# Table pieces behind the tile's transfers, and the second layer's first operand by halves

## The reference, cut to what matters

```python
# x: (128, 64, 1024) f32
x = x + L0_ffn(einsum('bct,bcd->bdt', x, W0[ids0]))     # 64x64 matrix for each batch entry, then
#   L0_ffn(y) = y @ W_base.T + b_base + 2 * sum_e gate_e * (y @ A_e.T) @ B_e.T   (top 2 of 8 experts, rank 16)
x = x + L1_ffn(x @ W1.T + base_bias + (x @ A[ids1].T) @ B[ids1].T)   # one of 32 adapters a batch entry, rank 16
#   L1_ffn(r) = fp8(r / s_in) @ fp8(Wf / s_w) * (s_in * s_w) + bias2
```

## Time and profile before

| | us |
|---|---|
| median of 3 runs | 2020.85 (2020.4 to 2025.44) |
| the profiled execution | 2019.35 |
| its span, first to last instruction | 2017.5 |
| PE busy | 1983.1 (98%) |
| DVE, POOL, ACT busy | 1490.1, 517.5, 393.9 |

### The profile page before, as it was taken

One profiled execution on the slowest core, in us unless ns is written; L12 is line 12 of the kernel. 1 busy time (PEld: TensorE's weight loads), 2 busy tenths in 40 slices (PEclk: granted clock), 3 DMA queues, 4 the chain that ended last, 5 costly groups with the idle time before them and its releaser, 6 DMA issues.

```text
span 2017.5 us, 38464 instructions
## 1 busy us (share of the span) xinstructions
PE 1983.1 (98%) x13056; PEld 1802.5 (89%) x13056; DVE 1490.1 (74%) x3882; ACT 393.9 (20%) x1084; POOL 517.5 (26%) x469
## 2 busy tenths in 40 slices
PE   6899999999999999999999999999999999999998
PEld 5889999999999999999988888888888888888887
DVE  6887877777766666666657777777777777777777
ACT  3112111111211111111112121212121222122211
POOL 3655411111111111111112222322232223222222
PEclk8999999999999999999999999999999999999999
DMA  7764443343333333333455566566656665665564
GB/s 241 226 192 140 135 122 107 104 126 116 101 111 110 98 97 116 106 96 113 123 162 151 163 166 161 152 168 164 163 148 173 160 161 149 173 159 161 155 171 111
DMA packets 220202, 289.93 MB, mean 144 GB/s; under 512 B 97795, under 2 KB 169477, under 8 KB 220166
## 3 DMA queue, kind: packets, MB, share of 16 engines
q1 hardware_dynamic: 220166, 289.56, 50.7%
HBM read 163.62 MB, written 109.05 MB: 135 GB/s over the span
## 4 chain that ended last, share of the span: by engine, by line
PE 93%; SPq 2%; DMA 2%; POOL 1%; DVE 1%; issue 0%; ACT 0%; DVEq 0%; ACTq 0%
PE bank_g L977 13%; PE bank_g L1032 12%; PE bank_g L979 12%; PE bank_g L978 12%; PE bank_g L1031 12%; PE bank_g L1030 12%; PE bank_f L1040 11%; PE bank_f L957 3%; PE bank_g L1075 1%; PE bank_g L1005 1%; PE bank_g L1006 1%; PE bank_g L1004 1%; DMA raw<-b 1%; DMA raw<-a 1%; POOL w1h L557 1%; POOL w1l L559 1%
## 5 line engine op out<-in xcount | busy, mean ns | idle before, releaser
L977 PE MATMUL bank_g<-w0h,st_h 128*128 128x384 f32 (+1 forms) x1536 | 529.7, 345 | 10.4 <-DMA wpair<-wc 6.5
L978 PE MATMUL bank_g<-w0l,st_h 128*128 128x384 f32 (+1 forms) x1536 | 520.7, 339 | 0.0
L979 PE MATMUL bank_g<-w0h,st_l 128*128 128x384 f32 (+1 forms) x1536 | 520.6, 339 | 0.0
L1030 PE MATMUL bank_g<-w1h,st_h 128*128 128x352 f32 x1536 | 506.1, 329 | 4.0 <-DVE st_l L882 4.0
L1032 PE MATMUL bank_g<-w1h,st_l 128*128 128x352 f32 x1536 | 496.7, 323 | 0.0
L1031 PE MATMUL bank_g<-w1l,st_h 128*128 128x352 f32 x1536 | 495.8, 323 | 0.0
L882 DVE TENSOR_TENSOR st_l<-xbuf,st_h 128x512 fp32r<-128x512 f32 x128 | 212.8, 1703 | 183.9 <-ACT st_h L676 183.9
L977 PEld LDWEIGHTS bank_g<-w0h,st_h 128*128 128x128 f32 x1536 | 289.5, 188 | 41.2 <-issue 26.1
L547 POOL TENSOR_TENSOR xbuf<-xbuf,b_base_sb 128x1024 f32<-128x1024 f32 x64 | 154.4, 2412 | 654.0 <-PE bank_f L957 640.4
L1030 PEld LDWEIGHTS bank_g<-w1h,st_h 128*128 128x128 f32 x1536 | 289.2, 188 | 11.9 <-DVE st_l L882 4.6
L1031 PEld LDWEIGHTS bank_g<-w1l,st_h 128*128 128x128 f32 x1536 | 289.0, 188 | 1.6
(11 more groups left out here) (79 smaller groups left out, 1988.8 us busy)
## 6 DMA issues: line engine op xcount, KB each, us to landing
xbuf<-x SPq DMA_DIRECT2D x64, 512.0 KB, 3.9
x_scratch<-x1buf SPq DMA_DIRECT2D x64, 512.0 KB, 2.9
x1t_scratch<-x_blocks SPq DMA_DIRECT2D x256, 128.0 KB, 2.3
xbuf<-x1t_scratch SPq DMA_DIRECT2D x64, 512.0 KB, 3.6
x1buf<-x_scratch SPq DMA_DIRECT2D x64, 512.0 KB, 5.1
out<-obuf SPq DMA_DIRECT2D x64, 512.0 KB, 2.7
b_stack<-b_split SPq DMA_DIRECT2D x384, 64.0 KB, 3.6
raw<-a_split SPq DMA_DIRECT2D x128, 128.0 KB, 4.2
```

What stands on the lines that cost most here:

```text
L977: pe.matmul(to, st_h[:, rows], w0h[:, k, cols], start=(k == 0), stop=False)
L978: pe.matmul(to, st_h[:, rows], w0l[:, k, cols], start=False, stop=False)
L979: last = pe.matmul(to, st_l[:, rows], w0h[:, k, cols], start=False, stop=(k == KC - 1))
L1030: pe.matmul(to, st_h[:, rows], w1h_k[:, k, cols], start=(k == 0), stop=False)
```

## The change

- `POOL_PIECES_A_TILE` is 2 instead of 3. In SP's loop `tile(t)` comes first and `feed(t)` behind it. The tables now take tiles 0 to 8 and the weight tiles 8 to 20.
- `base_bias` becomes a 17th table piece ("C", 128x8): POOL splits it in stage 1, SP stores it as `bias_split` in DRAM and loads both rows with one DMA to each `b_stack`. `bias_raw`, `bias_h`, `bias_l`, L471, L483 and the operations of ACT (L683) and DVE (L926) go.
- `st_used[h]` is counted in stage 2 too, at the last matmul of each half of k in group 2; ACT waits for it half by half instead of for `main_done`.
- `turned_lo(0, 0, h)` is done inside DVE's last stage 1 tile: half 0 ahead of the additions into `x1buf`, half 1 behind the first of them.
- POOL waits for `bias2` inside its `tile`, behind `fill_slot`.

```diff
-POOL_PIECES_A_TILE = 3
+POOL_PIECES_A_TILE = 2
...
+    bias_dram = nc.dram_tensor("bias_split", (2, D), F32, kind="Internal").ap()
...
+            pool_units += [("C", 0, 0)]
             tables = len(pool_units)
...
+                elif kind == "C":
+                    src = base_bias.rearrange("(p c) -> p c", p=P)
+                    to = [bias_dram[s].rearrange("(p c) -> p c", p=P) for s in range(2)]
...
                 for t in range(PREP_TILES):
+                    tile(t, t % 2, True)
                     feed(t)
-                    tile(t, t % 2, True)
...
-                sp.dma_start(bias_raw[:, :], base_bias.rearrange("(a n) -> a n", a=1)).then_inc(bias_loaded, 16)
+                for b in range(2):
+                    sp.dma_start(b_stack[b][3 * LR:STACK, :].bitcast(F32), bias_dram).then_inc(bias_rows, 16)
...
-                sp.wait_ge(bias_split, 2)
-                for b in range(2):
-                    for s, part in enumerate((bias_h, bias_l)):
-                        sp.dma_start(b_stack[b][3 * LR + s:3 * LR + s + 1, :].bitcast(F32),
-                                     part[:, :].bitcast(F32)).then_inc(bias_rows, 16)
...
-                pool.wait_ge(x1_done[2], TILES)
-                pool.wait_ge(bias2_loaded, 16)
                 def tile(t, b, x1_loads, a_loads, stored):
                     if a_loads is not None:
                         fill_slot(t + 1, 1 - b, a_loads)
+                    if stored is None:
+                        pool.wait_ge(x1_done[2], TILES)
+                        pool.wait_ge(bias2_loaded, 16)
...
-                        act.wait_ge(main_done, t)
                     for h in range(2):
+                        act.wait_ge(st_used[h], TILES + t)
                         act.activation(turned(st_h[:, :], h), in_blocks(xbuf[:, b, :], h), ACT.Copy)\
                            .then_inc(hi_done[h], 1)
...
                     if more:
                         st_lo(n, 0)
+                    else:
+                        turned_lo(0, 0, 0)
...
                         if g == 0 and more:
                             st_lo(n, 1)
+                        elif g == 0:
+                            turned_lo(0, 0, 1)
...
+                        if g == 2 and k % (KC // 2) == KC // 2 - 1:
+                            last.then_inc(st_used[k // (KC // 2)], 1)
...
-                        pe.wait_ge(bias_rows, 64)
+                        pe.wait_ge(bias_rows, 32)
```

More of the change, by code:

```diff
@@ L236, in pool_places @@
                     to = [b1_dram[u * P:(u + 1) * P, s, v * HALF:(v + 1) * HALF] for s in range(2)]
+                elif kind == "C":
+                    src = base_bias.rearrange("(p c) -> p c", p=P)
+                    to = [bias_dram[s].rearrange("(p c) -> p c", p=P) for s in range(2)]
+                    cols = slice(n * HALF, n * HALF + D // P)
+                    return src, D // P, w1h[:, cols], w1l[:, cols], to
                 else:
@@ L265, in build @@
             bias2_sb = sb("bias2_sb", [P, D], F32, p2)
-            bias_raw = sb("bias_raw", [1, D], F32, p2)
-            bias_h = sb("bias_h", [1, D], F32R, p2)
-            bias_l = sb("bias_l", [1, D], F32R, p2)
             x1_loaded = [sem(f"x1_loaded{b}") for b in range(2)]
@@ L274, in build @@
             bias2_loaded = sem("bias2_loaded")
-            bias_loaded = sem("bias_loaded")
-            bias_split = sem("bias_split")
             bias_rows = sem("bias_rows")
@@ L279, in build @@
             turned_loaded = [sem(f"turned_loaded{b}") for b in range(2)]
-            main_done = sem("main_done")
             masked_done = sem("masked_done")
@@ L668, in turned_hi @@
                     act.wait_ge(turned_loaded[b], 16 * loads)
-                    if isinstance(t, int) and t == 0:
-                        act.wait_ge(st_used[1], TILES)
-                    else:
-                        act.wait_ge(main_done, t)
                     for h in range(2):
+                        act.wait_ge(st_used[h], TILES + t)
                         act.activation(turned(st_h[:, :], h), in_blocks(xbuf[:, b, :], h), ACT.Copy)\
@@ L679, in _ @@
                 turned_hi(0, 0, 1)
-                act.wait_ge(x1_done[2], TILES)
-                act.wait_ge(bias_loaded, 16)
-                act.activation(bias_h[:, :], bias_raw[:, :], ACT.Copy).then_inc(bias_split, 1)
                 def tile(t, b, lag, loads):
@@ L753, in _, with turned_lo @@
                 dve.wait_ge(s_scale, 3)
+                def turned_lo(t, b, h):
+                    dve.wait_ge(hi_done[h], TILES + t + 1)
+                    dve.tensor_tensor(turned(st_l[:, :], h), in_blocks(xbuf[:, b, :], h),
+                                      turned(st_h[:, :], h), ALU.subtract).then_inc(lo_done[h], 1)
                 def quantize_weight(u):
@@ L877, in quantize @@
                        .then_inc(rq_done, 1)
[L879 to L884, removed]
                 def finish(t, b, bank=bank_f):
@@ L917, in tile @@
                     if more:
-                        turned_lo(t + 1, 1 - b)
-                turned_lo(0, 0)
+                        for h in range(2):
+                            turned_lo(t + 1, 1 - b, h)
                 dve.wait_ge(ones_set, 1)
                 dve.tensor_copy(ht[3 * LR:STACK, :], ones[3 * LR:STACK, :].to_broadcast([2, P])).then_inc(ht_ones, 1)
-                dve.wait_ge(bias_split, 1)
-                dve.tensor_tensor(bias_l[:, :], bias_raw[:, :], bias_h[:, :], ALU.subtract).then_inc(bias_split, 1)
                 tile(0, 0, 0, True)
@@ L1063, in main @@
                         last.then_inc(h1_ps, 1)
-                    if g == 2:
-                        last.then_inc(main_done, 1)
                 def stacks_in(t, b, loads):
```

## The result

The changed kernel takes 2014.34 us (median of 6 runs, 2011.4 to 2015.59) beside 2021.38 for the one before (6 runs, 2020.4 to 2025.44): a ratio of 0.996, with a 95% interval of 0.9947 to 0.9972. That is 7.0 us won where 13.7 were forecast, outside the range on record. The two profiled executions differ by less still: 2015.41 with a span of 2013.2 against 2019.35 and 2017.5, 4.3 us of span.

What follows compares the result with a forecast made beforehand. PE bounds the kernel, busy 1983.1 of 2017.5 us, so only its idle time and slow stretches can be won. The terms 8.99 - 0.3 + 5.0 = 13.7 us gave 2007.2 us, with a range of 2004 to 2013.

Steps and rivals of the forecast that it cites:

- Stage 1, what is removed: Stage 1, tiles 2 to 5: PE's waits for `wpair` and the slow restarts go, 8.99 us gained.
- Rival A: Stage 1: matrices late from table traffic, not order; 1 us a tile lost over 8 tiles, 2015; chance 0.12.
- Rival B: Stage 1: each of 9 tiles with table traffic costs 2.25 us, so the kernel is slower, 2027; chance 0.04.
- Stage 1, what is added: Stage 1, tiles 8 to 9: POOL waits for the last table piece's store; 0.3 us lost once (0 to 1.0).
- rival D: Stage 1: no effect worth measuring, waits go elsewhere, such as to `xb_done`; 2018 to 2021; chance 0.06.
- (1) to (3): Between the stages: PE gains 2.5 us at its start, 3.3 by L1075, 4.5 by tile 1, 6.1 with the clock.
- (4): Start of `ffn(0)`: a new wait of about 0.9 us for `rqt`; of 6.1 us gained 5.0 are kept.
- (3): Stage 2, tile 1: starts at 1026.8 instead of 1031.33, gain 4.5 us; 6.1 with the clock staying up.
- rival C: Between the stages: adapter B or transpose late, or clock falls; only 1 to 2.5 of 5.0 us stay, 2010.5; chance 0.14.

Runs made afterwards that it cites:

- the hold in all tiles: Changed kernel with POOL's pieces and next bias addition held in each tile until DVE has made `hwt`; 2007.15 us, ratio 0.9929 to the kernel before.
- after_again: The changed kernel run once more, unaltered; 2014.76 us, ratio 0.9971 to the kernel before.
- rest_alone: Changed kernel with three pieces a tile and `feed(t)` first, as before the change; 2019.16 us, ratio 0.9986 to the kernel before.

## Why the prediction was half right

**Stage 1, what is removed: right.** T(5) - T(1) is 61.82, forecast 61.3; 8.47 of 8.99. SP's queue in tile 1 of the changed kernel, T(1) being 58.29:

```profile
60.66 0.35 SPq L411 DMA_DIRECT2D x_scratch<-x1buf  x1
61.06 0.43 SPq L414 DMA_DIRECT2D xbuf<-x  x1
62.87 1.75 SPq L351 DMA_DIRECT2D wpair<-wc  x2
64.67 2.04 SPq L421 DMA_DIRECT2D x1t_scratch<-x_blocks  x4
66.75 0.46 SPq L398 DMA_DIRECT2D a_split<-w1h  x1
```

The store is at T + 2.4 as in the earlier trace rows, the second matrix load is out by T + 6.3, the table's stores stand behind L421. Rival A is out: the landing of `wpair` in this stretch is 2.3 (it was 2.8 in the earlier trace rows), so most of its slowness went with the order, and there is no matrix wait left to give back. The estimate by the Trainium skill (DMA: Bandwidth & Descriptors, on latency), from HBM's access time at high load, was a landing of 3.9; the 2.3 does not bear it out. Rival B needed 1.6 us of lateness a tile and had none. About half of what is missing from the 8.99 is POOL's: with the hold in all tiles, T(5) - T(1) is 61.5 to 61.6 in four traces.

**Stage 1, what is added: the named cost right, the unnamed one missed.** For piece 17 in tile 8 the sum took 0.3. The addition of the bias for tile 9 ends at 182.31, T(9) is at 181.84, and T(9) - T(8) is 15.43 against 15.33: 0.1. DVE waits 1.25 us for that addition, the sign that was named for rival D, but only there. The first step that failed is the sentence "The remaining idle time (the start, the end) is not touched by the change", and behind it "POOL does fewer pieces in a tile than before" and, in rival D, "8 us a tile to do in 15.3": the last two count POOL by its time. Its time was never short. What it costs is DVE's, where a two-input operation of POOL runs beside a DVE operation of the kinds above; and what DVE's delay costs depends on when it falls. In tile 0 it falls on the only chain for which PE stands still: 2.35 us, which no term of the sum held, though DVE's stretched operations (0.60 where 0.29 is free, 3.71 where 2.38 is) were there to see in the trace of before, and the sum didn't look into tile 0. In tiles 5 to 10, where 91.96 before was exactly the undisturbed pace, PE loses 1.74 instead of the 0.3 (2.6 in `after_again`). The hold shows it to be mostly POOL's, as said above; why POOL's larger work there cost nothing before was not followed operation by operation.

**Between the stages, (1) to (3): right.** Timeline of PE, the changed kernel:

```profile
1011.00 0.34 PE L994 MATMUL bank_g<-b0h,hwt 128*128 128x384 f32 x1
1011.18 0.32 PE L1018 MATMUL bank_g<-w1h,st_h 128*128 128x352 f32 x1
...
1022.90 0.70 PE L1064 MATMUL bank_g<-b_stack,ht 98*128 98x320 f32 x3
1024.09 0.40 PE L1018 MATMUL bank_g<-w1h,st_h 128*128 128x352 f32 x1 [0.48 <-ACT val L685]
...
1035.68 0.64 PE L1064 MATMUL bank_g<-b_stack,ht 98*128 98x320 f32 x3
```

PE goes from stage 1 to stage 2 without a gap; no wait ahead of L1064; tile 1 begins at T(63) + 14.10, forecast 14.35. In `rest_alone` and `after_again` L1064 does wait 1.2 and 1.0 for what the profile can only call issue: adapter B is as close as the sum had it, on one side or the other.

**(4), the second step that failed: the mechanism right, its size not.** SP comes to the transpose at 1033.96, T(63) + 24.0, near the forecast (1036.5 with T(63) at 1012.45 is + 24.05). It lands 4.2 later, not 3.1 to 3.7 as in the earlier trace rows, and PE waits 1.94 (2.7 and 2.8 in two other traces) instead of 0.9. Then the clock, which (3) expected to stay up, falls. Busy time of each engine, then the granted clock, DMA's share and GB/s, from 1035 to 1043 of the changed kernel:

```profile
1035.00:1043.00 8.00, 6.07 (x24) 2.87 (x23) 6.12 (x6) 1.94 (x4) 4.98 (x5) 0.79 0.40 46
```

A mean of 0.79 is 0.42 of the stretch at the lower of the two levels (1.2 GHz), 3.4 us, and half of that is lost: 1.7 us, and the 16 matmuls took 5.31 where they take 3.63 at full clock, 1.68. So in this trace the term cost 3.6 us where 0.9 was taken, and instead of 5.0 the stretch up to the end of `ffn(0)` gave 4.29 - 1.68 = 2.6. The low clock does not repeat, the size of the gain does: in `after_again` L1064 waits 0.98 and `ffn(0)` 2.72, the clock stays up, and from T(63) to `ffn(62)` it wins 3.1 us, as does the first trace (991.99 less 988.91); `rest_alone` wins 2.8. In all three 0.4 to 0.5 of it comes in the tiles behind `ffn(0)`, which the prediction had as worth nothing. That is close to rival C, which had 1 to 2.5 of 5.0 staying, and the whole would by C have been 2010.5; the rest to 2014.3 is for the most part tile 0 and tiles 5 to 10.

**The sum again.** 13.7 forecast; less 0.5 (T(1) to T(5)), 4.25 (start: 1.90 of later begin, 2.35 of chain), 1.4 (tiles 5 to 10 beyond the 0.3), 2.4 (`rqt` and clock), 0.8 (behind `ffn(0)`: 1.24 at the end, of it 1.00 a second wait ahead of L1040, less 0.47 won in the tiles between): 4.3, what the two spans differ by. The 1.90 goes with the landing of one load, and the second wait ahead of L1040 stands in five of the ten traces that have the changed second stage without the hold at its end; what remains without the 1.90 and the 0.8 is 7.0, which is what the medians show. That the two agree to a tenth is chance; both are uncertain by a microsecond or two. The span of `after_again` lies 5.1 us below that of before; without the 1.23 of its later start that is 6.3. The range failed since every term in it was one that the change names. Nothing in it stood for work that the change moves next to other work elsewhere.

## What to carry to other kernels

Before work is moved or thinned out on GpSimd, ask which chain on VectorE it will now run beside, above all in the first tile, where TensorE has nothing else to do; an engine that is busy a quarter of the time can still set the end. Have a look at the stretches that the change doesn't name, and put a term for them in the sum. A queue that issues in program order is best sorted by first use: of the four orders tried, three took one wait away, had another one and brought no gain in the ratio.

## What was not expected of the hardware

- A GpSimd operation holds up VectorE operations far smaller than itself: 128x2 took 1.27 instead of 0.22 us, a cast of 128x128 1.17 instead of 0.23, a difference of 128x128 2.33 instead of 0.29. Beside a GpSimd TENSOR_SCALAR (L557, 31.07 to 32.57 before) the same difference took 0.60: slowed, and not held to the end. The stretched ones ended with a GpSimd TENSOR_TENSOR.
- A wait inside GpSimd's program, which does nothing but hold it back, made the whole kernel faster by 7.2 us by medians, 6 to 8.5 by ratios.
- The transpose of `rq` landed 4.2 us after its issue at the start of stage 2; over all of stage 2 the median is 3.7 (2.6 to 4.4).
- The clock didn't follow the length of a wait alone. After 1.94 us of it the 16 matmuls of `ffn(0)` took 5.31 us. In `rest_alone` 15 of them, behind a longer wait, were at full speed, and so it was in `after_again` behind 2.72; what tells them apart is open:

```profile
1042.59 3.40 PE L1031 MATMUL bank_f<-wq,rqt 128*128 128x512 bf16 x15 [2.81 <-DMA rqt<-rq]
```
